# Leaving out the nine identity products per pass in a four-stage recurrent kernel

## The chip, the cores and the metric

The kernel runs on one core of a Trainium2 chip. The metric is the device time of one execution in microseconds. Time before the change: 4627.35 us, the median of 3 runs (4625.21 to 4628.95).

## What is computed

The input x has 4 sequences of 1024 tokens and 512 features. Four layers follow each other, each added to the stream:

```
x = x + rnn(x)        # h_t = tanh(x_t Wx + b + h_(t-1) Wh), 512 wide
x = x + ssm(x)        # conv over 4 taps, projections, softplus/tanh, a scan with 64 states, Wo
x = x + lstm(x)       # A = x_t Wx + b + h_(t-1) Wh (2048 wide), sigmoid/sigmoid/sigmoid/tanh gates
x = x + adapted(x)    # x times (base layer + low-rank part made from the condition vector)
```

Both the RNN and the LSTM are strictly sequential over 1024 tokens. All is float32; the recurrent weights and states are split into two float16 parts each.

## The kernel before

The 1024 tokens are cut into 32 chunks of 32 tokens (CT = 32, NCH = 32), and the four layers form a pipeline over chunks. A pass i handles chunk i in the RNN, chunk i-1 in the state-space layer ("mid"), chunk i-2 in the LSTM and chunk i-3 in the output layer; `chunk_work(i)` says which of them run. There are 35 passes, 0 to 34. Passes 0 to 3 are written out, passes 4 to 29 stand in a hardware loop of two passes an iteration (`pipeline`, `eng.Fori`, line 226 in the trace), so that 12 jumps back lie between them, and passes 30 to 34 are written out again. The LSTM runs in passes 2 to 33, the RNN in 0 to 31. Passes 2 to 31 are the 30 that run both; the windows below are taken from them.

Inside a pass every engine goes through the same 32 steps, one token of RNN and LSTM each. On TensorE a step s is, in program order:

- the LSTM products (L898): 64 matrix instructions with 256 moving columns, four at a time in column tiles. The first half waits for `lstm_h_ready0`, the rest for `lstm_h_ready1`, that is for VectorE's h of the step before (L753);
- the RNN products (L926): 32 instructions, behind `rnn_h_ready`;
- a filler that depends on s: the output layer (L938, steps 1, 2, 6, 13), the transposition of the next chunk (L1003, step 0), the state-space projections (L957, steps 3 to 5; those of step 4 wait for the convolution made on ScalarE and GpSimd), the RNN's input products (L1009, steps 7 to 10), the identity products (L972, steps 11, 30, 31), the state-space output (L977, step 12, behind `y_ready`), and the LSTM's input products (L991, steps 14 to 29).

TensorE, ScalarE, VectorE and GpSimd are joined by semaphores alone; there is no planner, the order is the one written by hand. VectorE transposes the LSTM's sums out of PSUM (L716), reduces them (L722), ScalarE makes the gates (L491) and tanh of the cell (L496), and VectorE makes products, cell and h (L728 to L753). In step 11 VectorE also runs the state-space scan, which waits for GpSimd. At the end of a pass each engine waits for a `go` from the SyncE queue (`next_chunk`).

The identity products multiply the 128 x 128 identity by itself into the fourth quarter of `psS`, which nothing reads:

```
HOLD_STEPS = [11, 30, 31]
...
if s in HOLD_STEPS:
    for _ in range(3):
        mm(psS[:, 3 * TOK:4 * TOK], ident[:, :], ident[:, :], start=True, stop=True)
```

They have no wait of their own, nobody waits for them, and they are issued in all 35 passes, also where the LSTM or the RNN is not at work. A float32 product is recorded as two matrix instructions and two weight loads.

Of the kernel before, what the change touches and what calls it, by code (L numbers as in the profile page):

```python
# [18 lines left out]
TOK = NB * CT  # L19
# [25 lines left out]
OUT_STEPS = [1, 2, 6, 13]  # L45
CONV_STEPS = [0, 1, 2, 2]
SSM_STEP = 3
HOLD_STEPS = [11, 30, 31]
L0_STEP = 7
RECIP_STEP = 7  # L50
RECIP_CUTS = [0, 40, 88, TOK]
# [25 lines left out]
def resid_stack_kernel(nc, x, cond, l0_Wx, l0_Wh, l0_b, conv_b, Wp, bp, Ws, bs, A_log, dt_log, Wo, bo,  # L77
                       l2_Wx, l2_Wh, l2_b, base, w1, b1, w2, b2, ln_g, ln_b, out):
    ctx = ExitStack()
    with ctx:  # L80
        def sb(name, shape, dt=F32):
            return ctx.enter_context(nc.sbuf_tensor(name, shape, dt))

        def pb(name):
            return ctx.enter_context(nc.psum_tensor(name, [P, 512], F32))
# [34 lines left out]
        ident = sb("ident", [P, P])  # L120
# [9 lines left out]
        def hidden(v):  # L130
# [53 lines left out]
        psL0, psL1, psR, psOut, psX, psS, psA, psB = [pb(n) for n in  # L184
            ("ps_lstm0", "ps_lstm1", "ps_rnn", "ps_out", "ps_x", "ps_ssm", "ps_lstm_in_a", "ps_lstm_in_b")]
# [643 lines left out]
        def _(pe):  # L829
            mm = nc.tensor.matmul  # L830
# [38 lines left out]
            for q in range(W2R):  # L869
# [4 lines left out]
                for k in range(KB):  # L874
                    for c in range(NQ):
                        last = mm((psA, psB)[q % 2][QC * c:QC * c + NB, 0:wd], hmT[:, k, :], w2s[q % 2][:, k, wd * c:wd * (c + 1)],
                                  start=(k == 0), stop=(k == KB - 1), tile_position=(0, QC * c))
# [11 lines left out]
            def body(_i, par, _known, w, p):  # L889
                S, S_last = sets[par], sets[1 - par]  # L890
                for s in range(CT):
# [26 lines left out]
                    if w["rnn"]:  # L918
# [4 lines left out]
                        for k in range(KB):  # L923
                            for e in range(2):
                                for j in range(NQ):
                                    last = mm(psR[QC * j:QC * j + LO + NB, 0:RW], hrs[:, k, :], whr[:, k, e, j, :],  # L926
                                              start=(k == 0 and e == 0), stop=(k == KB - 1 and e == 1), tile_position=(0, QC * j))
# [3 lines left out]
                    if w["out"] and s in OUT_STEPS:  # L931
# [5 lines left out]
                        for n in range(NB):  # L937
                            last = mm(psOut[CT * n:CT * (n + 1), :], x3s[1 - par][:, k, :, n], layer[:, n, k, :],  # L938
                                      start=(k == 0), stop=(k == KB - 1), tile_position=(0, CT * n))
# [8 lines left out]
                    if w["mid"] and SSM_STEP <= s < SSM_STEP + 3:  # L948
# [5 lines left out]
                        for k in range(KB):  # L954
# [3 lines left out]
                                      start=(k == 0), stop=(k == KB - 1))  # L958
                        if c == 1:
                            last.then_inc(S["ssm_mm"], 1)  # L960
                    if w["l0"] and L0_STEP <= s < L0_STEP + KB:
# [5 lines left out]
                            last = rnn_in(mm, wxr, xT[1 - par], psI, s - L0_STEP, k)  # L967
                        if s == L0_STEP + KB - 1:
                            last.then_inc(S["l0_mm"], 1)
                    if s in HOLD_STEPS:  # L970
                        for _ in range(3):
                            mm(psS[:, 3 * TOK:4 * TOK], ident[:, :], ident[:, :], start=True, stop=True)  # L972
                    if w["mid"] and s == WO_STEP:
                        pe.wait_ge(S["y_ready"], 1)
                        for b in range(KB):
# [3 lines left out]
                    if w["mid"] and s >= L2_STEP:  # L979
                        for u in range(L2_MM * (s - L2_STEP), min(L2_MM * (s - L2_STEP + 1), L2_ALL)):  # L980
# [7 lines left out]
                            if g >= 2 and b == 0 and k == 0:  # L988
# [3 lines left out]
                                      start=(k == 0), stop=(k == KB - 1))  # L992
                            if b == KB - 1 and k == KB - 1:
                                last.then_inc(S["l2_mm"], 1)
                next_chunk(pe, "pe")

            pipeline(pe, body)


# [74 lines left out]
```

## Time and profile before

| | us |
|---|---|
| median of 3 runs | 4627.35 |
| the profiled execution | 4620.95 |
| its span, first to last instruction | 4618.9 |
| TensorE products, busy | 3707.8 (80%) |
| TensorE weight loads, busy | 2997.8 (65%) |
| VectorE busy | 3678.6 (80%) |
| ScalarE busy | 1530.7 (33%) |
| GpSimd busy | 1283.4 (28%) |
| mean granted TensorE clock | 0.960 of full |

The profile is of one execution. Busy shares say how much an engine did, not whether it set the time. The granted clock is a share of TensorE's full 2.4 GHz; 0.5 is 1.2 GHz, and a value between them for a stretch means that part of it was at either. The timeline merges the instructions of one line that follow each other, so that a step's 64 LSTM products are one row; "idle before" is the idle time of the engine before the first of them, with what ended it. A row of the windows view gives, for a stretch A:B, its length, then busy us and number of instructions of TensorE's products, its weight loads, VectorE, ScalarE and GpSimd, then the granted clock, the share of the DMA engines and GB/s. A window of a step reaches from the start of its LSTM products to the start of the next ones.

### The profile page before, as it was taken

The numbers are of one execution on the slowest core, as the hardware profiler recorded it, in microseconds if no ns is written. First come the engines' busy times: TensorE is split into PE (matmuls) and PEld (weight loads), VectorE is DVE, ScalarE is ACT, GpSimd is POOL, SyncE is SP. The second block draws the span as 40 slices with busy tenths as digits, with TensorE's granted clock in tenths as the row PEclk, the third lists the DMA queues.
The fourth block names the chain that finished last, engine by engine and source line by source line (L and its number), as shares of the span: only waits on it lengthen the run. The fifth ranks groups of instructions, "written<-read, shape, count | busy, mean of one in ns | idle before, by whom it ended". The sixth has DMA issues, their size and how long they took to land.

```text
span 4618.9 us, 252593 instructions
## 1 busy us (share of the span) xinstructions
PE 3707.8 (80%) x106846; PEld 2997.8 (65%) x106846; DVE 3678.6 (80%) x20952; ACT 1530.7 (33%) x6667; POOL 1283.4 (28%) x4520
## 2 busy tenths in 40 slices
PE   4557888888888888888888888888888888888875
PEld 4246667676666666666666666666666766666653
DVE  5337888888888888888888888888888888888866
ACT  0013333333333333333333333333333333333321
POOL 0023332223333323233332223333223233333221
PEclk6579999999999999999999999999999999999999
DMA  4300000000000000000000000000000000000000
GB/s 152 117 4 6 8 6 8 9 8 6 9 8 7 8 9 8 7 9 8 9 6 9 8 8 7 8 9 8 7 8 9 6 8 9 8 4 6 6 5 7
DMA packets 28394, 64.27 MB, mean 14 GB/s; under 512 B 11068, under 2 KB 11708, under 8 KB 26120
## 3 DMA queue, kind: packets, MB, share of 16 engines
q1 hardware_dynamic: 27144, 46.99, 3.2%
q8 instruction: 860, 14.09, 1.3%
q14 instruction: 390, 3.19, 0.2%
HBM read 38.45 MB, written 8.39 MB: 10 GB/s over the span
## 4 chain that ended last, share of the span: by engine, by line
DVE 39%; PE 33%; ACT 10%; POOL 8%; issue 7%; DMA 1%; SPq 1%; DVEq 0%; POOLq 0%; ACTq 0%
PE ps_lstm L898 29%; DVE lstm_sums L716 10%; DVE lstm_arg L722 6%; DVE lstm_h_scaled L745 4%; ACT lstm_gates_2c L491 4%; ACT lstm_tanh_c L496 3%; DVE lstm_gates_2c L733 3%; POOL stage L378 3%; DVE lstm_ig_fc L728 2%; POOL stage L379 2%; DVE lstm_h_parts L753 2%; DVE rnn_h_parts L817 2%; DVE lstm_h_parts L749 2%; DVE rnn_arg L781 2%; DVE lstm_o_scaled L737 2%
## 5 line engine op out<-in xcount | busy, mean ns | idle before, releaser
L898 PE MATMUL ps_lstm<-lstm_Wh_parts,lstm_h_parts 128*20 128x256 f16 x65536 | 2039.9, 277 | 660.4 <-DVE lstm_h_parts L753 615.5
L898 PEld LDWEIGHTS ps_lstm<-lstm_Wh_parts,lstm_h_parts 128*20 128x20 f16 x65536 | 1508.2, 92 | 1182.8 <-DVE lstm_h_parts L753 932.7
L716 DVE STREAM_TRANSPOSE lstm_sums<-ps_lstm 128x256 f32<-128x256 f32 x2048 | 913.0, 446 | 180.7 <-PE ps_lstm L898 135.3
L491 ACT ACTIVATE lstm_gates_2c<-lstm_arg 128x32 f32<-128x32 f32 x2048 | 470.9, 230 | 1660.8 <-DVE lstm_arg L722 1660.0
L353 POOL COPY lstm_sums<-lstm_in 128x32 f32<-128x32 f32 x2048 | 412.5, 211 | 1408.0 <-DVE lstm_arg L722 1394.2
L926 PE MATMUL ps_rnn<-rnn_Wh_parts,rnn_h_parts 128*20 128x128 f16 x32768 | 651.1, 222 | 73.6 <-DVE rnn_h_parts L819 71.0
L926 PEld LDWEIGHTS ps_rnn<-rnn_Wh_parts,rnn_h_parts 128*20 128x20 f16 x32768 | 552.9, 93 | 117.6 <-DVE rnn_h_parts L819 97.9
L722 DVE TENSOR_REDUCE lstm_arg<-lstm_sums 128x32 f32<-128x96 f32 x2048 | 535.6, 262 | 106.7 <-DVE lstm_o_scaled L737 0.6
L496 ACT ACTIVATE lstm_tanh_c<-lstm_gates_2c 128x8 f32<-128x8 f32 x2048 | 413.1, 202 | 392.5 <-DVE lstm_gates_2c L733 384.8
L516 ACT ACTIVATE rnn_h<-rnn_arg 128x16 f32<-128x16 f32 x1024 | 221.1, 216 | 929.6 <-DVE rnn_arg L781 929.6
L817 DVE TENSOR_SCALAR rnn_h_parts<-rnn_h 128x16 f16<-128x16 f32 x1024 | 237.7, 232 | 291.1 <-ACT rnn_h L516 291.1
L728 DVE SCALAR_TENSOR_TENSOR lstm_ig_fc<-lstm_gates_2c 128x16 f32<-128x16 f32 x2048 | 368.8, 180 | 31.1 <-ACT lstm_gates_2c L491 31.0
L753 DVE TENSOR_TENSOR lstm_h_parts<-lstm_h_scaled,lstm_h_parts 128x8 f16<-128x8 f32 x2048 | 358.3, 175 | 37.4 <-DVE lstm_h_parts L749 2.4
L775 DVE STREAM_TRANSPOSE rnn_sums<-ps_rnn 128x128 f32<-128x128 f32 x1024 | 315.2, 308 | 62.9 <-PE ps_rnn L926 62.8
L733 DVE SCALAR_TENSOR_TENSOR lstm_gates_2c<-lstm_ig_fc 128x8 f32<-128x8 f32 x2048 | 364.1, 178 | 0.5 <-DVE lstm_h_scaled L745 0.2
L745 DVE TENSOR_TENSOR lstm_h_scaled<-lstm_o_scaled,lstm_tanh_c 128x8 f32<-128x8 f32 x2048 | 341.8, 167 | 3.4 <-DVE lstm_ig_fc L728 0.5
L737 DVE TENSOR_SCALAR lstm_o_scaled<-lstm_gates_2c 128x8 f32<-128x8 f32 x2048 | 340.0, 166 | 2.6
L365 POOL COPY rnn_sums<-rnn_in 128x16 f32<-128x16 f32 x512 | 100.5, 196 | 832.1 <-DVE rnn_arg L781 604.2
L749 DVE TENSOR_TENSOR lstm_h_parts<-lstm_o_scaled,lstm_tanh_c 128x8 f16<-128x8 f32 x2048 | 328.3, 160 | 0.3 <-issue 0.2
L991 PE MATMUL ps_lstm_in_a<-x,lstm_Wx 128*128 128x128 f32 x2048 | 298.2, 289 | 0.0
L991 PE MATMUL ps_lstm_in_b<-x,lstm_Wx 128*128 128x128 f32 x2048 | 296.5, 288 | 0.0
L365 POOL COPY rnn_sums<-stage 128x16 f32<-128x16 f32 x512 | 100.5, 196 | 653.0 <-DVE rnn_arg L781 586.2
(156 smaller groups left out, 3474.7 us busy)
## 6 DMA issues: line engine op xcount, KB each, us to landing
stage<-in_L_cond_w SPq DMA_DIRECT2D x8, 2048.0 KB, 8.0
x_rows<-in_x SPq DMA_DIRECT2D x32, 256.0 KB
out<-out_rows SPq DMA_DIRECT2D x128, 64.0 KB, 1.9
stage<-in_L_cond_Wh SPq DMA_DIRECT2D x1, 4096.0 KB, 12.7
lstm_Wx<-in_L_cond_Wx SPq DMA_DIRECT2D x1, 4096.0 KB, 13.3
stage<-in_L_cond_Wh SPq DMA_DIRECT2D x1, 1024.0 KB, 5.7
rnn_Wx<-in_L_cond_Wx SPq DMA_DIRECT2D x1, 1024.0 KB, 7.9
stage<-in_L_cond_w SPq DMA_DIRECT2D x1, 1024.0 KB, 15.1
```

Source lines behind the costliest of these rows:

```text
L491: A.activation(gate[h][:, 0:G, :].rearrange("p g q -> p (g q)"), arg[h][:, :, :].rearrange("p g n -> p (g n)"), ACT.Tanh, scale=gate_scale ...
L496: A.activation(tc[h][:, :], cell[h], ACT.Tanh, scale=0.5).then_inc(S[f"lstm_tanhc{h}"], 1)
L716: return mark(V.transpose(tr[h][s % 2][:, :, 0:QC], psL[h][:, 0:HW].rearrange("p (g c) -> p g c", c=QC)))
L722: V.tensor_reduce(arg[h][:, :, :], three.rearrange("p g s n -> p g n s"), AX.X, ALU.add).then_inc(S[f"lstm_summed{h}"], 1)
L728: return mark(V.scalar_tensor_tensor(out=prod[h][:, :, :], in0=gate[h][:, 0:2, :], scalar=1.0, in1=gate[h][:, G - 1:G + 1, :], op0=ALU.add ...
L733: V.scalar_tensor_tensor(out=cell[h], in0=prod[h][:, 1, :], scalar=0.5, in1=prod[h][:, 0, :], op0=ALU.mult, op1=ALU.add).then_inc(S[f"lstm ...
L737: return mark(V.tensor_scalar(o_s[h][:, :], gate[h][:, 2, :], 1.0, H_SCALE, ALU.add, ALU.mult))
L745: at = mark(V.tensor_tensor(half(hl, h)[:, :, s, :], o3, t3, ALU.mult))
L753: V.tensor_tensor(half(hls, h)[:, :, LO:LO + NB], half(hl, h)[:, :, s, :], half(hls, h)[:, :, 0:NB], ALU.subtract).then_inc(S[f"lstm_h_rea ...
L898: ins = mm(psL[h][QC * j:QC * j + LO + NB, 0:HW], hls[:, k, :], whl[:, k, h, e, j, :], start=(k == 0 and e == 0), stop=(k == KB - 1 and e ...
L926: last = mm(psR[QC * j:QC * j + LO + NB, 0:RW], hrs[:, k, :], whr[:, k, e, j, :], start=(k == 0 and e == 0), stop=(k == KB - 1 and e == 1) ...
L991: last = mm((psA, psB)[g % 2][:, TOK * b:TOK * (b + 1)], w_, x2[:, k, :, :].rearrange("p t n -> p (t n)"), start=(k == 0), stop=(k == KB - 1))
```

## The change

The nine identity products of each pass, three in each of steps 11, 30 and 31, are left out, and the constant with them. Nothing else changes.

```
-HOLD_STEPS = [11, 30, 31]
...
-                    if s in HOLD_STEPS:
-                        for _ in range(3):
-                            mm(psS[:, 3 * TOK:4 * TOK], ident[:, :], ident[:, :], start=True, stop=True)
```

## Rows read from the trace of the kernel before

**Rows 1.** The page, parts 1 and 2: busy us; clock in tenths.
```profile
PE 3707.8 (80%) x106846; PEld 2997.8 (65%) x106846; DVE 3678.6 (80%) x20952; ACT 1530.7 (33%) x6667; POOL 1283.4 (28%) x4520
...
PEclk6579999999999999999999999999999999999999
```

**Rows 2.** The page, parts 4 and 5: chain by engine, costliest group.
```profile
DVE 39%; PE 33%; ACT 10%; POOL 8%; issue 7%; DMA 1%; SPq 1%; DVEq 0%; POOLq 0%; ACTq 0%
...
L898 PE MATMUL ps_lstm<-lstm_Wh_parts,lstm_h_parts 128*20 128x256 f16 x65536 | 2039.9, 277 | 660.4 <-DVE lstm_h_parts L753 615.5
```

**Rows 3.** Timeline of TensorE, an ordinary step (start us, us, line).
```profile
2050.71 1.93 PE L898 MATMUL ps_lstm<-lstm_Wh_parts,lstm_h_parts 128*20 128x256 f16 x64 [0.33 <-DVE lstm_h_parts L753]
...
2054.51 1.93 PE L898 MATMUL ps_lstm<-lstm_Wh_parts,lstm_h_parts 128*20 128x256 f16 x64 [0.33 <-DVE lstm_h_parts L753]
```

**Rows 4.** Timeline of TensorE, around steps 11, 12 and 30 of the same pass.
```profile
2015.36 0.94 PE L972 MATMUL ps_ssm<-ident 128*128 128x128 f32 x6
2018.66 0.62 PE L898 MATMUL ps_lstm<-lstm_Wh_parts,lstm_h_parts 128*20 128x256 f16 x16 [2.37 <-DVE lstm_h_parts L753]
2019.60 1.49 PE L898 MATMUL ps_lstm<-lstm_Wh_parts,lstm_h_parts 128*20 128x256 f16 x48 [0.32 <-DVE lstm_h_parts L753]
...
2093.15 1.93 PE L898 MATMUL ps_lstm<-lstm_Wh_parts,lstm_h_parts 128*20 128x256 f16 x64 [0.56 <-DVE lstm_h_parts L753]
```

**Rows 5.** Answer on line 972: durations in ns; nobody waited.
```profile
L972 PE MATMUL ps_ssm<-ident x630: 275/275/582, 238.8 to 4615.7; 128*128 128x128 f32 x158
...
who waited for it (us, times):
```

**Rows 6.** Timeline of TensorE in the first pass (clock halved).
```profile
285.45 1.04 PE L926 MATMUL ps_rnn<-rnn_Wh_parts,rnn_h_parts 128*20 128x128 f16 x32 [1.48 <-DVE rnn_h_parts L819]
286.42 1.65 PE L972 MATMUL ps_ssm<-ident 128*128 128x128 f32 x6
```

**Rows 7.** Chain of work that ended last, at its end.
```profile
4612.57 0.87 PE ps_ssm L972 x6
4613.44 1.03 PE ps_out L938 x8
```

**Rows 8.** Timeline of TensorE at a loop jump.
```profile
1959.80 0.28 PE L972 MATMUL ps_ssm<-ident 128*128 128x128 f32 x1
1963.47 3.46 PE L898 MATMUL ps_lstm<-lstm_Wh_parts,lstm_h_parts 128*20 128x256 f16 x64 [3.39 <-issue]
```

**Rows 9.** Answer on line 226: TensorE's sequencer branches (ns).
```profile
L226 PEldq COMPARE_BRANCH  x13: 76/4255/4780, 892.5 to 4089.3; - x13
```

**Rows 10.** Windows, step 12 of passes 4, 29 and 31.
```profile
681.76:687.26 5.50, 5.17 (x106) 4.12 (x106) 4.35 (x27) 2.38 (x9) 1.03 (x4) 0.69 0.01 1
...
4012.51:4016.87 4.36, 3.63 (x104) 2.94 (x104) 3.87 (x24) 2.37 (x9) 1.02 (x4) 1.00 0.00 0
...
4273.61:4279.16 5.55, 5.08 (x104) 3.75 (x104) 4.05 (x24) 0.98 (x5) 1.02 (x4) 0.69 0.02 4
```

**Rows 11.** Windows, step 0 of passes 6, 12, 20 and 21.
```profile
896.70:901.60 4.90, 3.60 (x104) 3.08 (x104) 2.48 (x16) 0.77 (x4) 0.42 (x2) 1.00 0.03 10
...
1698.15:1704.22 6.07, 6.07 (x104) 4.74 (x105) 3.00 (x18) 0.77 (x4) 0.45 (x3) 0.53 0.03 8
...
2762.48:2767.67 5.19, 4.85 (x105) 3.67 (x105) 2.53 (x15) 0.77 (x4) 0.42 (x2) 0.72 0.03 9
2895.75:2899.55 3.80, 3.46 (x104) 2.97 (x104) 3.33 (x21) 0.98 (x5) 1.64 (x9) 1.00 0.03 6
```

**Rows 12.** Timeline of TensorE, the product that waits for the convolution.
```profile
1986.09 1.09 PE L957 MATMUL ps_ssm<-stage,ssm_Wp 128*64 128x128 f32 x8 [2.15 <-POOL stage L371]
```

**Rows 13.** Windows, step 5 of passes 28 and 29.
```profile
3850.80:3856.25 5.45, 5.04 (x105) 3.77 (x104) 3.09 (x19) 0.98 (x5) 0.62 (x3) 0.69 0.02 3
3982.77:3986.57 3.80, 3.39 (x105) 2.92 (x104) 2.94 (x18) 0.99 (x5) 0.62 (x3) 1.00 0.02 6
```

**Rows 14.** Timeline of TensorE, near the end, steps with only an LSTM.
```profile
4593.72 1.93 PE L898 MATMUL ps_lstm<-lstm_Wh_parts,lstm_h_parts 128*20 128x256 f16 x64 [1.87 <-DVE lstm_h_parts L753]
```

## Prediction

> **What bounds the kernel now.** I read the page first for busy shares: TensorE 80%, VectorE 80%, neither full, and a granted clock that is 9 tenths or more after the opening [rows 1]. Two engines at 80% with nothing near 100% is the sign of a chain that hands work back and forth. The chain of waits says so: VectorE 39%, TensorE 33%, ScalarE 10% of the span, and the costliest group is the LSTM product of L898, whose 660.4 us of idle time before it end, for 615.5 us, with VectorE's h parts (L753) [rows 2]. So the time is the recurrence, one step after the other: products, transpose, reduce, tanh, cell, h, products.
>
> Then the timeline of TensorE, to see what lies in a step. In an ordinary one the LSTM products start at 2050.71, take 1.93 us, and the next ones start at 2054.51: 3.80 us a step. A filler (L991, the next pass's input product) ends 0.33 us before the next start [rows 3]. TensorE's work behind the LSTM products is thus hidden, with 0.33 us to spare. What sits on the path is the 1.93 us, and that is the part which depends on TensorE's clock.
>
> **What the change removes.** Three identity products in each of steps 11, 30 and 31 of each of 35 passes: 630 recorded matrix instructions (2 x 9 x 35), which is six for each group of three; such a six takes 0.94 us at full clock, from the start of its first to the end of its last in the merged timeline, and 1.65 us at half clock [rows 5, 6]. Nobody reads their output: no engine waits for them [rows 5]. Nothing is added or moved, no wait changes.
>
> **Direct cost, step by step.** Steps 30 and 31: the products end and TensorE idles 0.56 us until the h parts come [rows 4]. Removing them makes that wait about 1.4 us and moves nothing: 0. Step 11: TensorE idles 2.37 us behind them [rows 4]; VectorE is held there by the scan of the state-space layer, which waits for GpSimd. Removing 0.94 us of TensorE work in front moves nothing either: 0. In the last pass three of them stand in the chain that ends last, 0.87 us in front of the last output product [rows 7]: -0.87. In the first pass, where the clock is halved and there is no LSTM, a group takes 1.65 us where the step before had 1.48 us of idle [rows 6]: 0.17 us too much, once or twice, bounds 0 and -0.34, taken -0.2.
>
> The loop jump: every second pass TensorE's sequencer spends 4.26 us (median) in the branch [rows 9], and the LSTM products start when it ends. Counted back from the start at 1963.47, that branch began near 1959.1, when the last identity products (the final one starts 1959.80 [rows 8]) had hardly begun. So the sequencer runs ahead of the engine, and only the issue of the twelve instructions (six loads, six products), not their 0.9 us, can delay it. Bounds: 0 and -0.85 us at each of 12 jumps, -10.2. I take -0.1 x 12 = -1.2, near the first end, since the branch already overlaps the products.
>
> **Indirect cost: the clock.** This is where I expect the time. The identity products are the only TensorE work in some gaps, and the windows show what follows a gap. In passes 2 to 31, step 12 takes 4.36 or 4.37 us at granted clock 1.00 in 25, and 5.49 to 5.55 us at 0.69 in 5 (the ones at 681.76, 814.59, 951.29, 4142.74 and 4273.61, of which first and last stand in the rows) [rows 10]. A clock of 0.69 over the step means that part of it ran at 1.2 GHz rather than 2.4 GHz; the price is 5.49 - 4.36 = 1.13 us. What TensorE did before the fall is the same gap of 2.2 to 2.4 us after the step 11 products. So with the products in place this gap already costs a fall in 5 passes of 30. Without them the gap is 2.37 + 0.94 = 3.31 us.
>
> What follows a gap of that size? The gap at the loop jump is 3.39 us in [rows 8], and 11 of 12 jumps show a lower clock in step 0: 5.19 us at 0.72 where the pass without a jump has 3.80 us at 1.00; the one that escaped was the first, 4.90 us at 1.00 [rows 11]. The gap of 2.15 us in front of a product that waits for the convolution [rows 12] is followed by a slow step 5 (5.45 us at 0.69 against 3.80) in ten of the eleven even passes from 1188.72 to 3850.80 and in none of the odd ones between them [rows 13]. So after 2.2 us the clock falls sometimes, after 3.4 us nearly always. At 3.31 us I take it that step 12 falls in all 25 passes that now escape: 25 x 1.13 = +28.3.
>
> How long the slow stretch lasts is the next question. The cover in step 12 is thinner than in step 0: 0.32 us idle inside its LSTM products [rows 4]. The jump at 1698.15 shows what a slow stretch that is followed by another costs: 6.07 us at 0.53 [rows 11]. At step 12 a second stretch would fall on step 13, an ordinary step, and the nearest price of an ordinary step at the lower clock is step 5's, 5.45 - 3.80 = 1.65 us [rows 13]. Bounds: never, 0; always, 30 x 1.65 = 49.5. Eleven jumps fell and one had a second stretch, but there TensorE is busier after the fall; I take one pass in three, 10 x 1.65 = +16.5.
>
> At the jump the gap grows from 3.4 to about 4.3 us, so the fall lies earlier and more of step 0 is slow. Bounds: 0 and 6.07 - 5.19 = 0.88 us at 12 jumps, 10.6 [rows 11]. I take 0.3 x 12 = +3.6. Steps 30 and 31 where no jump follows have 1.4 us of idle in 3.8, less than a step with only an LSTM product (1.87 us idle in the last passes [rows 14]), where the page's clock still shows 9 tenths [rows 1]: 0.
>
> A rule of the Trainium skill bears on this. The row shows a slow step 0 of 5.19 us against 3.80, +1.39 us [rows 11]. The page "TensorE: Matmul & The Clock Gate", section "HAM oscillation — how this bites in real kernels", says that an idle wait between bursts returns the engine to half rate, so that the next burst starts cold each time; the row agrees that the fall follows the gap. By the page's half rate the whole LSTM product of step 12 would take 1.93 us more, 25 x 1.93 = 48 us instead of the 28.3 above (an estimate from the page's rule and [rows 3]), and the sum would be 4693. The rows decide for 1.13, since only part of the step is slow.
>
> **Sum.** -0.9 - 0.2 - 1.2 + 28.3 + 16.5 + 3.6 = +46.1 us. The profiled execution had 4620.95 us (span 4618.9 and 2.05 around it): 4667. The median of the three runs is 6.4 us above it, so on that footing 4627.35 + 46.1 = 4673.4 us, +1.0%.
>
> **The rivals.**
> *No change.* The identity products keep nothing up: the fall at step 12 depends on where the gap happens to lie against the clock's own rhythm, and as many passes fall as now. For it: 5 passes fall with the products in place, and the last odd passes before the end do not fall at the conv gap of the same size. Against it: the 3.4 us gaps. Then only -0.9 - 0.2 - 1.2 is left: 4625 us.
> *Faster.* The sequencer is held by the queue behind the identity products, so that each branch begins the whole 0.85 us sooner: 12 x 0.85 = 10.2, with the last pass 11.1 to 11.3: 4616 us. For it: the branch starts about when the first of them does. It decides only if step 12 does not fall in more than about ten further passes (10 x 1.13 = 11.3); from there the clock wins.
> *Much slower.* The slow state feeds itself: step 13 falls in every pass and step 0 is slow throughout, 28.3 + 49.5 + 10.6 - 2.3 = +86: 4713 us. A step with only an LSTM, as in the last pass but one, could also stay slow. Against it: all but one of the falls at jumps were over within the step.
>
> **How the numbers follow.** Forecast, step 12 falls nearly everywhere and step 13 in part: 0.74. Much slower: 0.10. No change: 0.09. Faster: 0.07. The likeliest case's own range is 4650 to 4700: below, step 13 never falls and the jump costs nothing, 4673 - 20 = 4653; above, half of the passes more, +1.65 x 15 = 25. The range for 8 in 10 goes from 4645 to 4706, which leaves out the no-change and the faster case and most of the much slower one. 0.2% of the time, 9 us, is about what a measurement of this kernel can tell from no change. Slower by more than that: 0.74 + 0.10 = 0.84. Within: 0.09 and some of the faster case (its 11 us is just outside), 0.10. Faster: 0.06.
>
> **What the profile of the changed kernel would show.** Right: L972 gone; the idle time before step 12's LSTM products 3.2 to 3.3 us; granted clock about 0.7 in the windows of step 12 in at least 25 passes of 30 with 5.5 us each; a slow step 13 in some; the mean granted clock down from 0.960; the pair of passes between jumps longer by about 3.5 us. Wrong: step 12 at 4.36 us and clock 1.00 in most passes (then the gap is still covered); a loop gap shorter by 0.8 us (then the queue held the branch); step 12 slow but step 11's stall on GpSimd swallowing the loss later, so that the pass is no longer; or step 13 slow everywhere.

## The result

The changed kernel takes 4667.23 us, the median of 4 runs (4662.29 to 4668.49), against 4626.28 us before (4 runs, 4619.68 to 4628.95). The ratio is 1.0089, 95% interval 1.0071 to 1.0106: slower by 0.9%, about 41 us. The profiled execution took 4668.49 us, its span is 4666.7 us, 47.7 us more than before.

From the page of the changed kernel: busy time, the clock in 40 slices, the chain by engine, and the costliest group (all lines behind the diff have moved up by one, so L897 is the L898 of [rows 2]).

```profile
PE 3672.4 (79%) x106216; PEld 2959.1 (63%) x106216; DVE 3679.2 (79%) x20952; ACT 1532.0 (33%) x6667; POOL 1284.4 (28%) x4520
...
PEclk6569999999999999999999999999999999999999
...
DVE 37%; PE 36%; ACT 10%; POOL 8%; issue 7%; DMA 1%; SPq 1%; DVEq 0%; POOLq 0%; ACTq 0%
...
L897 PE MATMUL ps_lstm<-lstm_Wh_parts,lstm_h_parts 128*20 128x256 f16 x65536 | 2068.3, 279 | 739.4 <-DVE lstm_h_parts L752 674.7
```

TensorE does less (630 recorded matrix instructions gone, two for each of 315 products) and yet has a larger share of the chain, 36% against 33% in [rows 2]; the same 65536 LSTM products take 2068.3 us instead of 2039.9. The 40 slices hardly show it; the mean granted clock does, 0.944 against 0.960. The idle time before the products grew too, by 79 us, so the clock is not all.

To see where the time lies, one window for each step s of the 30 passes, and the sums over them. The windows of step 12 of the changed kernel, four of 30 and the sum:

```profile
958.38:964.60 6.22, 6.21 (x105) 4.68 (x106) 4.53 (x27) 2.51 (x10) 1.12 (x5) 0.53 0.01 4
1091.97:1096.34 4.37, 3.64 (x105) 2.95 (x105) 3.88 (x24) 2.38 (x9) 1.03 (x4) 1.00 0.02 4
...
2036.74:2041.89 5.15, 4.81 (x104) 3.42 (x104) 4.05 (x24) 2.38 (x9) 1.02 (x4) 0.73 0.02 5
2167.62:2173.11 5.49, 5.17 (x104) 4.18 (x104) 4.43 (x27) 2.38 (x9) 1.03 (x4) 0.69 0.01 3
...
sum 154.88, PE 142.48 PEld 109.79 DVE 124.82 ACT 70.91 POOL 31.43; mean PE 4.75 PEld 3.66 DVE 4.16 ACT 2.36 POOL 1.05
```

19 of 30 are at a lower clock (5 before), and the sum is 154.88 us against 136.62 in the same view of the kernel before [rows 10]: +18.3. The sum before:

```profile
sum 136.62, PE 116.68 PEld 94.30 DVE 118.62 ACT 69.99 POOL 30.84; mean PE 3.89 PEld 3.14 DVE 3.95 ACT 2.33 POOL 1.03
```

Step 0, the step behind the loop jump, one window at a jump, one without, and the sum of 30:

```profile
1981.37:1988.74 7.37, 6.36 (x105) 4.87 (x106) 3.01 (x18) 0.77 (x4) 0.42 (x2) 0.54 0.03 8
2115.82:2119.62 3.80, 3.47 (x104) 2.95 (x104) 3.33 (x21) 0.98 (x5) 1.63 (x9) 1.00 0.03 6
...
sum 159.98, PE 135.51 PEld 108.22 DVE 94.92 ACT 28.32 POOL 35.37; mean PE 4.52 PEld 3.61 DVE 3.16 ACT 0.94 POOL 1.18
```

Against 131.18 before: +28.8, and 28.2 of it at the 12 jumps (7.1 to 8.2 us each; 4.9 to 6.1 before, [rows 11]). The sum of step 31, which holds the jump, fell from 148.41 to 140.81: -7.6. Step 0 before, then step 31 before and in the changed kernel:

```profile
sum 131.18, PE 119.61 PEld 97.19 DVE 90.70 ACT 26.86 POOL 34.45; mean PE 3.99 PEld 3.24 DVE 3.02 ACT 0.90 POOL 1.15
...
sum 148.41, PE 97.25 PEld 81.75 DVE 109.50 ACT 70.45 POOL 20.99; mean PE 3.24 PEld 2.73 DVE 3.65 ACT 2.35 POOL 0.70
...
sum 140.81, PE 71.33 PEld 59.53 DVE 109.36 ACT 70.56 POOL 20.97; mean PE 2.38 PEld 1.98 DVE 3.65 ACT 2.35 POOL 0.70
```

Steps 4 and 5 gave +4.8 and -0.7. With 2.3 us before the first LSTM product, 2.6 in passes 32 and 33 and -1.0 at the end that is 47.5 of the 47.7; the other steps nearly cancel.

The timeline of TensorE at one jump of the changed kernel says what step 0 is made of:

```profile
1977.30 0.62 PE L925 MATMUL ps_rnn<-rnn_Wh_parts,rnn_h_parts 128*20 128x128 f16 x32
1981.37 2.06 PE L897 MATMUL ps_lstm<-lstm_Wh_parts,lstm_h_parts 128*20 128x256 f16 x34 [3.45 <-issue]
1984.44 1.88 PE L897 MATMUL ps_lstm<-lstm_Wh_parts,lstm_h_parts 128*20 128x256 f16 x30 [1.01 <-issue]
1985.91 1.27 PE L925 MATMUL ps_rnn<-rnn_Wh_parts,rnn_h_parts 128*20 128x128 f16 x32
1987.11 1.70 PE L999 MATMUL ps_x<-ident,x_rows 128*128 128x128 f32 x8
```

There is a second hole. Behind the 34th of the 64 LSTM products TensorE idles 1.01 us, waiting for nothing that the profile shows ("issue"). It is at the 34th at all 12 jumps, 0.9 to 2.3 us long, and at none in the kernel before, where the 64 stand in one row [rows 8]. Nearly half of the extra time lies at the jump, with a cause that the prediction had not looked at.

### The profile page after: what moved, and what is told of

It is laid out like the page before. It is cut to its first block, busy times and chain, and to the rows that moved or that the text cites. A ratio compares the mean times of both kernels' runs of the same rounds, so it can differ in the third digit from the quotient of the medians.

```text
span 4666.7 us, 251333 instructions
## 1 busy us (share of the span) xinstructions
PE 3672.4 (79%) x106216; PEld 2959.1 (63%) x106216; DVE 3679.2 (79%) x20952; ACT 1532.0 (33%) x6667; POOL 1284.4 (28%) x4520
## 4 chain that ended last, share of the span: by engine, by line
DVE 37%; PE 36%; ACT 10%; POOL 8%; issue 7%; DMA 1%; SPq 1%; DVEq 0%; POOLq 0%; ACTq 0%
PE ps_lstm L897 31%; DVE lstm_sums L715 10%; DVE lstm_arg L721 6%; DVE lstm_h_scaled L744 4%; ACT lstm_gates_2c L490 4%; ACT lstm_tanh_c L495 3%; DVE lstm_gates_2c L732 3%; POOL stage L377 2%; POOL stage L378 2%; DVE lstm_h_parts L752 2%; DVE lstm_ig_fc L727 2%; DVE rnn_h_parts L816 2%; DVE lstm_h_parts L748 2%; PE ps_rnn L925 2%; DVE lstm_o_scaled L736 2%
## 5 line engine op out<-in xcount | busy, mean ns | idle before, releaser
L897 PE MATMUL ps_lstm<-lstm_Wh_parts,lstm_h_parts 128*20 128x256 f16 x65536 | 2068.3, 279 | 739.4 <-DVE lstm_h_parts L752 674.7
L897 PEld LDWEIGHTS ps_lstm<-lstm_Wh_parts,lstm_h_parts 128*20 128x20 f16 x65536 | 1520.2, 93 | 1273.7 <-DVE lstm_h_parts L752 989.8
L925 PE MATMUL ps_rnn<-rnn_Wh_parts,rnn_h_parts 128*20 128x128 f16 x32768 | 665.1, 225 | 76.0 <-DVE rnn_h_parts L818 74.5
L925 PEld LDWEIGHTS ps_rnn<-rnn_Wh_parts,rnn_h_parts 128*20 128x20 f16 x32768 | 565.9, 95 | 121.3 <-DVE rnn_h_parts L818 101.5
```

Source lines behind the costliest of these rows:

```text
L897: ins = mm(psL[h][QC * j:QC * j + LO + NB, 0:HW], hls[:, k, :], whl[:, k, h, e, j, :], start=(k == 0 and e == 0), stop=(k == KB - 1 and e ...
```

## The experiments

Each time is a median of 5 or 11 runs beside 9 to 21 runs of the kernel before on the same chip. Windows, timelines and counts of slow passes (a pass is slow in a step where the clock granted in that window is below full) come from the one profiled execution of each kernel. The identity products feed nothing, so none of these kernels leaves out part of the computation. "Short products" are identity products with 4 moving columns, put into the set-up in front of the wait for the low-rank factors' DMA:

```
+            for _ in range(N):
+                mm(psS[:, 3 * TOK:3 * TOK + 4], ident[:, :], ident[:, 0:4], start=True, stop=True)
             pe.wait_ge(d_xab, 16 * 2 * NQ * NB)
```

**36 short products ahead of the loop (e1_pad36).** The changed kernel with N = 36, as many products as the change takes out of passes 0 to 3.

> The changed kernel, with 36 short identity products (4 moving columns) put into the set-up before the loop, behind the low-rank weight products where TensorE waits for a DMA: as many as the change takes out of passes 0 to 3. The loop body stays without any. In the changed kernel every step 0 behind a loop jump stops after its 34th LSTM product for 0.9 to 2.3 us, idle that is put down to issue; the kernel before never does. Placement theory: that stop is instruction supply, and depends on where the loop begins in the program; with 36 products put back ahead of it the stop is gone, step 0 behind a jump falls from 7.1-8.1 us to 5.0-6.1, and the time falls by 12 x 1.5 to 2.2 = 18 to 26 us, to 4641-4650. Cover theory (the missing products in step 31 let the gap grow and the clock fall earlier, and nothing else): the stop stays, step 0 stays above 7 us, and the time stays at 4667 within 4.

4630.08 us (11 runs, 4623.93 to 4636.65) against 4620.71 (21 runs), ratio 1.0020, 1.0011 to 1.0029. The timeline at a jump:

```profile
1429.95 0.62 PE L928 MATMUL ps_rnn<-rnn_Wh_parts,rnn_h_parts 128*20 128x128 f16 x32
1434.08 3.58 PE L900 MATMUL ps_lstm<-lstm_Wh_parts,lstm_h_parts 128*20 128x256 f16 x64 [3.51 <-issue]
1437.46 0.65 PE L928 MATMUL ps_rnn<-rnn_Wh_parts,rnn_h_parts 128*20 128x128 f16 x32
```

The hole in the LSTM products is gone, step 0 at the jumps is 5.2 to 6.1 us, and three quarters of the loss with it: 1.0020 in place of 1.0089. It went below the range of the placement theory (4641 to 4650): step 31 also lost 10.2 us against before. The cover theory is out for step 0. What stays is step 12: 24 of 30 passes at a lower clock, +20.0 us. The sums of its step 0 and step 12:

```profile
sum 135.33, PE 126.22 PEld 103.25 DVE 91.74 ACT 27.32 POOL 34.86; mean PE 4.21 PEld 3.44 DVE 3.06 ACT 0.91 POOL 1.16
...
sum 156.61, PE 144.66 PEld 112.43 DVE 125.64 ACT 70.96 POOL 31.56; mean PE 4.82 PEld 3.75 DVE 4.19 ACT 2.37 POOL 1.05
```

**9 short products (e2_pad9).** The changed kernel with N = 9.

> The changed kernel with 9 short identity products put ahead of the loop instead of 36. Placement theory with a fixed size of what is there after a jump: 9 products are 36 instructions of loads and products if each float32 product counts four times, so 18 LSTM products: the stop moves from behind product 34 to behind product 52 (43 if a product counts twice). It comes about 0.5 us later behind the jump and more of it is covered: step 0 6.5 to 7.6 us, the time 4655 to 4667. Cover theory: the stop stays behind product 34, or has nothing to do with a number of products; 4667.

4662.76 us against 4620.71, 1.0085 (1.0071 to 1.0099). The time lies in the expected range, but not for the reason given. At a jump:

```profile
1436.39 0.61 PE L900 MATMUL ps_lstm<-lstm_Wh_parts,lstm_h_parts 128*20 128x256 f16 x16 [3.80 <-issue]
1439.64 2.74 PE L900 MATMUL ps_lstm<-lstm_Wh_parts,lstm_h_parts 128*20 128x256 f16 x48 [2.63 <-issue]
```

The hole moved by 18 products, as said, but to the front: behind the 16th, not the 52nd, and it is longer (2.0 to 2.6 us). So 9 products ahead are 36 instructions, and they take from what is there after a jump, they do not add to it. I had the direction wrong. That fits a block with fixed borders: the more code lies ahead of the loop, the later in its block the loop begins, and the fewer of its instructions came with the first fetch.

**Identity products out of passes 0 to 3 alone (e3_head_out).**

```
-                    if s in HOLD_STEPS:
+                    if s in HOLD_STEPS and _known not in (0, 1, 2, 3):
```

> The kernel before with the identity products left out in passes 0 to 3 alone; the loop and the passes behind it keep all of them. Placement theory: the loop now begins where it does in the changed kernel, so the stop behind product 34 appears in the kernel that has its cover: step 0 behind a jump 6 to 7.5 us rather than 5.0-5.3, 12 x 1 to 2 us, and passes 2 and 3 cost 5.6 us more as in the changed kernel: 4640 to 4658. Cover theory: only passes 2 and 3 change, 4627 + 5.6 = 4632.

4638.17 us against 4620.71, 1.0040 (1.0026 to 1.0054). The hole behind the 34th product is there (1.24 us), in a loop that has all its identity products:

```profile
1434.39 2.10 PE L898 MATMUL ps_lstm<-lstm_Wh_parts,lstm_h_parts 128*20 128x256 f16 x34 [2.72 <-issue]
1437.72 1.88 PE L898 MATMUL ps_lstm<-lstm_Wh_parts,lstm_h_parts 128*20 128x256 f16 x30 [1.24 <-issue]
```

That is a little below the expected range and well above the rival's 4632: steps 5 and 31 gave 9.5 and 7.7 us back, while step 12 cost 8.1, with 13 slow passes, two of them passes 2 and 3. Step 0 sums to 160.68 us, as in the changed kernel, while the gap before it at the jumps is only 2.4 to 3.0 us. The missing cover in steps 30 and 31 is not needed for a step 0 above 7 us.

**Only step 11's products, only those of steps 30 and 31 (e4_hold11, e5_hold3031).** `HOLD_STEPS = [11]` with N = 24, and `HOLD_STEPS = [30, 31]` with N = 12, so that the loop begins at the same place in both as before. Where it ends still moves, since its body is shorter: by 48 and by 24 instructions (four for each identity product: two matrix instructions and two weight loads).

> The three products of step 11 kept in all passes, those of steps 30 and 31 left out, and 24 short ones put ahead of the loop so that it begins where it did before. It asks what the products of steps 30 and 31 are worth apart from placement. If they keep the clock up at the jump, step 0 is slower than before by 0.5 to 1.5 us at 12 jumps: 4633 to 4645. If they do nothing, or if their absence lets the jump start 0.6 us earlier at no cost (step 31 was 0.63 us shorter in the changed kernel), 4619 to 4629. Step 12 is slow in 4 to 8 passes of 30 either way, as before (5).

> The products of steps 30 and 31 kept in all passes, those of step 11 left out, and 12 short ones put ahead of the loop so that it begins where it did before. With placement equal the changed kernel was 9.4 us slower than before (4630.1 against 4620.7), and by steps its trace showed +20 us in step 12 (24 slow passes of 30 against 5) against -10 in step 31. If step 12's fall is due to the missing products of step 11 alone, this one shows 20 to 28 slow passes in step 12 and +18 to +24 us there, and is slower than before by 15 to 25 us where step 31 stays as before, or by 8 to 12 if the jump is shorter here too. Rival: the falls at step 12 come from where the whole pass lies against the clock's changes, and without a shorter step 31 they stay at 5 to 10: within 5 us of before.

Without steps 30 and 31: 4624.86 us against 4620.71, 1.0010 (1.0001 to 1.0019). Step 0 +2.6, step 12 +2.3 with 7 slow passes, step 31 +3.5, where the branch takes 4.52 us instead of 4.26; the time is that of the second case, products that do nearly nothing. The gap at the jump is 4.2 to 5.0 us here, and step 0 at the jumps grew by only 0.17 us each. Without step 11: 4651.13 against 4626.89, 1.0061 (1.0047 to 1.0075), and step 12 has 23 slow passes of 30. The windows of passes 6 to 8 and the sum for step 12 of the latter:

```profile
958.09:964.22 6.13, 6.13 (x104) 4.54 (x104) 4.52 (x27) 2.42 (x10) 1.03 (x5) 0.53 0.00 1
1091.55:1095.91 4.36, 3.64 (x104) 2.95 (x104) 3.87 (x24) 2.38 (x9) 1.02 (x4) 1.00 0.01 4
1227.46:1232.55 5.09, 4.74 (x106) 3.38 (x106) 4.06 (x24) 2.38 (x9) 1.02 (x4) 0.75 0.01 2
...
sum 160.04, PE 149.93 PEld 114.12 DVE 126.64 ACT 70.88 POOL 31.37; mean PE 5.00 PEld 3.80 DVE 4.22 ACT 2.36 POOL 1.05
```

160.04 - 136.62 = +23.4 us: the three products of step 11 are what keeps the clock up in step 12, and they carry nearly all that the nine are worth. The rival that the falls need a shorter step 31 is out: step 31 is 3.3 us longer in sum here. The idle time before step 12's products is now 3.10 or 3.23 us, from pass to pass, where it was 2.23 or 2.37 [rows 4]. The count of slow passes wanders: 4 to 13 of 30 in the seven kernels that keep the step 11 products in the loop (5, 13, 7 and 10 where the gap is as before), 19 to 24 in the five that do not. The two groups stay apart, but a difference of a few passes inside one says little.

**64 short products (e6_pad64).** The changed kernel with N = 64.

> The changed kernel with 64 short identity products ahead of the loop. 9 products moved the stop behind the jump from the 34th LSTM product to the 16th, 18 products of 2 instructions each for 9 x 4 = 36 instructions; 36 products moved it to where the 90th product of the step would be. If the supply comes in fixed blocks of 256 instructions (16384 bytes, as the packets of the instruction queue are), 64 products are one whole block and the stop is behind product 34 again, the time 4655 to 4670. Rival: what counts is only how much code lies ahead, or that something was put there at all; then the stop is elsewhere or gone and the time near 4630.

4662.29 us against 4626.89, 1.0082 (1.0068 to 1.0096), and the hole is behind the 34th product again:

```profile
1445.01 2.10 PE L900 MATMUL ps_lstm<-lstm_Wh_parts,lstm_h_parts 128*20 128x256 f16 x34 [3.78 <-issue]
1447.89 1.88 PE L900 MATMUL ps_lstm<-lstm_Wh_parts,lstm_h_parts 128*20 128x256 f16 x30 [0.79 <-issue]
```

64 x 4 = 256 instructions are one period. With the others: 34 products left without padding, 34 - 18 = 16 with 9, 34 - 72 + 128 = 90 with 36, 34 - 128 + 128 = 34 with 64. The kernel before has the same 90 as e1_pad36, and in it the hole is in the RNN products, behind 64 + 26, at the one jump that did not fall in clock (the 4.90 us at 1.00 of [rows 11]); at the jumps that fell, in both kernels, none can be seen:

```profile
896.70 1.92 PE L898 MATMUL ps_lstm<-lstm_Wh_parts,lstm_h_parts 128*20 128x256 f16 x64 [3.22 <-issue]
898.45 0.56 PE L926 MATMUL ps_rnn<-rnn_Wh_parts,rnn_h_parts 128*20 128x128 f16 x26
900.30 0.28 PE L926 MATMUL ps_rnn<-rnn_Wh_parts,rnn_h_parts 128*20 128x128 f16 x6 [1.30 <-issue]
```

**More cover (e7_cover).** The other way: in the loop passes 5 products ahead of the wait for the convolution, 6 in step 11, and 3 long ones ahead of the jump.

```
+                        if c == 0 and _known is None:
+                            for _ in range(5):
+                                mm(psS[:, 3 * TOK:4 * TOK], ident[:, :], ident[:, :], start=True, stop=True)
                         if c == 0:
                             pe.wait_ge(S["conv_ready"], KB)
...
-                        for _ in range(3):
-                            mm(psS[:, 3 * TOK:4 * TOK], ident[:, :], ident[:, :], start=True, stop=True)
+                        wide = _known is None and par == 1 and s == CT - 1
+                        for _ in range(6 if _known is None and s == 11 else 3):
+                            if wide:
+                                mm(psS[:, :], ident[:, :], layer[:, 0, 0, :], start=True, stop=True)
+                            else:
+                                mm(psS[:, 3 * TOK:4 * TOK], ident[:, :], ident[:, :], start=True, stop=True)
```

> The kernel before with more cover, in the loop passes only, so that the loop begins where it did: 5 identity products in step 4 ahead of the wait for the convolution, 6 instead of 3 in step 11, and in step 31 of the odd pass, ahead of the jump, 3 products with 512 moving columns instead of 128. Clock theory: gaps of 2.15, 2.4 and 3.4 us shrink to about 0.6, 1.4 and 1.4; the falls at steps 5, 12 and 0 vanish, 11 x 1.4 at the jumps, 13 x 1.2 to 1.6 at step 5 and 5 x 1.1 at step 12, in all 36 to 42 us: 4580 to 4586. Rival: the long products delay the branch or the first LSTM products behind it, or the sequencer's queue, and step 31 or 5 grows by more than step 0 gains: 4615 to 4640.

4590.34 us (4585.70 to 4595.38) against 4626.89, ratio 0.9927, 0.9914 to 0.9941: faster than both kernels, 36.5 us below the kernel before, and 4 us above the expected range. The timeline at a jump, then step 0 and the sum of step 5:

```profile
1415.49 2.84 PE L977 MATMUL ps_ssm<-layer_plus_2I,ident 128*128 128x512 f32 x6
1419.00 1.93 PE L898 MATMUL ps_lstm<-lstm_Wh_parts,lstm_h_parts 128*20 128x256 f16 x64 [0.66 <-issue]
1420.75 0.56 PE L926 MATMUL ps_rnn<-rnn_Wh_parts,rnn_h_parts 128*20 128x128 f16 x26
1422.15 0.28 PE L926 MATMUL ps_rnn<-rnn_Wh_parts,rnn_h_parts 128*20 128x128 f16 x6 [0.84 <-issue]
```

```profile
1419.00:1423.86 4.86, 3.69 (x105) 3.10 (x105) 2.44 (x15) 0.77 (x4) 0.42 (x2) 1.00 0.05 12
```

```profile
sum 115.22, PE 103.00 PEld 88.64 DVE 90.65 ACT 29.34 POOL 18.26; mean PE 3.43 PEld 2.95 DVE 3.02 ACT 0.98 POOL 0.61
```

No step 0 at a jump and one step 5 (of pass 30, behind the loop) is at a lower clock now, 11 and 13 before. Step 5 gave -16.4 us, step 4 -3.0, step 0 -6.6, step 31 -7.0. The last is not the clock's: the branch takes 3.58 us instead of 4.26, and the loop's end has moved by 64 instructions; with the same cover and another end the next two runs have branches of 4.20 and 3.81 us. That leaves some 29 of the 36 us to the cover. Step 12 gave only -1.2: the doubled cover, a gap of 1.6 to 1.7 us, left 4 slow passes where 5 had been, all four of them inside the loop. Step 0 kept more than the expectation left it, 4.4 to 5.0 us at full clock, because the hole behind the 90th product is now in the open.

**More cover and 45 or 59 short products (e8_cover_pad45, e9_cover_pad59).**

> The kernel with more cover and 45 short identity products ahead of the loop, which by blocks of 256 instructions puts the loop's first instruction at the start of a block (180 instructions further than before: 90 products of 2 left become 128). The stop that stood behind product 90 of step 0 in one pass of the kernel before cannot occur in step 0. If the jump fetches one block before it goes on, nothing else changes: within 3 us of the kernel with more cover alone. If what lies behind in the block also sets the length of the branch, step 31 changes by up to 0.8 us at 12 jumps, 10 us either way.

> More cover, with 59 short identity products ahead of the loop. The last expectation had the sign of the count wrong: products ahead of the loop take from what is left of the block behind the jump, so 45 left nothing (step 31 with the jump took 9.8 to 10.4 us, two fetches in a row). With 59, 90 - 118 + 128 = 100 products of the loop's first block are left, more than the 96 LSTM and RNN products of step 0, so the stop of 0.7 to 1.1 us behind the 90th is gone from the RNN products. The end of the loop moves by 300 instructions against the kernel before, that is 44 of a block of 256. Over ten kernels the branch took 4.1 to 5.1 us where that end was shifted by -48 to 0 and 3.3 to 4.15 where by +36 to +184 (counted modulo 256). Block theory: branch 3.3 to 4.1, no stop, 4580 to 4591, at best 8 us below more cover alone (4590). Rival: placement matters only where the stop hits the LSTM products, since RNN products have slack: the same time within 3 us.

With 45: 4652.80 us against 4626.89, 1.0060 (1.0046 to 1.0073), slower than before in spite of all its cover.

```profile
1430.07 2.84 PE L979 MATMUL ps_ssm<-layer_plus_2I,ident 128*128 128x512 f32 x6
1438.12 3.60 PE L900 MATMUL ps_lstm<-lstm_Wh_parts,lstm_h_parts 128*20 128x256 f16 x64 [5.21 <-issue]
```

I had used the direction that the run with 9 had already refuted. By the right count 90 - 90 = 0 products of the first block are left, and that is what stands here: 5.21 us of idle in place of 0.66, since the first LSTM product of the loop comes with the second fetch. 12 x 3.9 = 47 us, the step 31 sum being 188.04 against 141.47 with more cover alone. All 12 step 0 are at a lower clock again, which costs 9.6 us more. It is the worst place of those run.

With 59: 4587.52 us against 4625.48, 0.9917 (0.9903 to 0.9931). The hole behind the 100th product, as computed, can be seen at 4 of the 12 jumps (0.15 to 0.28 us), and step 0 lost 4.3 us against more cover alone, but step 31 gave 1.9 back. The two intervals overlap; the 2.8 us between them are not shown to be a gain.

**46 short products in the kernel before (e10_pad46).**

> The kernel before, all nine identity products kept, with 46 short ones ahead of the loop: 126 products of the first block are left behind the jump, and the end of the loop is shifted by 184 of 256 instructions, the same as in the kernel with 36 products ahead and none in the loop, whose branch took 3.3 to 3.9 us. Theory that the place of the loop's end in its block sets the length of the branch: 3.3 to 3.9 us instead of 4.1 to 4.8, 12 x 0.65 = 8 us less in step 31, of which the clock at step 0 and 12 may give or take some: 4612 to 4622. Rival: the branch is shorter in those kernels because the loop holds fewer instructions or something else that was changed in each: branch 4.1 to 4.8 and 4623 to 4630.

4622.65 us against 4625.48 (11 and 15 runs), 0.9992, 0.9982 to 1.0002. TensorE's branches of the kernels, each line min/median/max in ns: the changed kernel, then only step 11's, then this one:

```profile
L225 PEldq COMPARE_BRANCH  x13: 76/3810/4073, 899.2 to 4135.1; - x13
```

```profile
L226 PEldq COMPARE_BRANCH  x13: 76/4524/5104, 899.7 to 4097.5; - x13
```

```profile
L226 PEldq COMPARE_BRANCH  x13: 76/3462/3822, 890.3 to 4079.9; - x13
```

The branch is shorter as forecast (3.46 against the 4.26 us of [rows 9]) with the same loop body, and step 31 lost 9.9 us, while step 12 gave 5.4 back (10 slow passes instead of 5). That execution's span is 7.8 us below the one of the kernel before, as forecast; but it is the fastest of the 11, and the medians differ by only 2.8 us, between the two expected ranges. So the length of the branch follows the place, and a gain in time is not shown.

## Why the prediction was right, and which of its steps were not

The direction and the size hold (forecast 4673, range 4645 to 4706, measured 4667). The working does not hold as well as the total.

*Steps 11, 30 and 31 are off the path:* right. No step with or without them changed by its own TensorE work: step 30, and step 31 where no jump follows, take 3.80 us in both kernels. The end gave -1.0 us, -0.87 said. The 0.2 us said for the first pass can't be seen: the first LSTM product comes 368.1 to 371.8 us into the span over the twelve profiled executions, with no order by the products left out.

*Step 12 falls in clock, at 1.13 us each:* right in mechanism, shown by the run that leaves out step 11's products alone. Mis-sized: not all 25 further passes fell but 14 (19 of 30), and with placement restored 19 (24 of 30). The price was near the 1.13 us said in 13 of the 19 (5.09 to 5.55 against 4.36 us, 0.7 to 1.2) and 1.8 us in the other six (6.12 to 6.21 us, at 0.53), so 18.3 us came of 14 further passes where 1.13 each would give 15.8.

*A second slow stretch on step 13 in one pass of three, +16.5:* wrong. Step 13 is slow in none (in one pass each of the runs with 9 and 64 short products, +1.4 and +1.5 us). Steps 12 and 13 together were forecast at 44.8 us and gave 18.3.

*The branch begins 0.1 us sooner:* right, 0.08 us (its start lies 2.17 instead of 2.25 us behind the start of step 31's LSTM products). But the branch was also 0.45 us shorter in the median, and step 31 gave -7.6 where -1.2 stood. The faster rival had 10.2 us there, for another reason.

*The jump costs 0.3 us more, +3.6:* this step failed. It reads the gap as TensorE's idle time and the clock behind it, and takes the code behind the jump as given. Step 0 gave +28.8, and in the run where the place of the loop's beginning is restored it gave +4.2. The rest is the hole in the instruction supply. The gap did not grow to 4.3 us either: its median over the jumps went from 3.35 to 3.66 us, because the branch became shorter; in the run with step 11's products alone, where the branch takes 4.52 us, it is 4.53. Each step 0 at a jump grew by 2.35 us where the hole has 1.4 in the mean; with it the clock is lower, 0.50 to 0.62 where it was 0.70 to 0.74 in ten of twelve. That TensorE stays low for longer because it idles once more is likely, but only argued.

So the 0.9% are the sum of three things. With the loop's beginning in its old place the change costs 0.20% (0.11 to 0.29), 9 us, and that is a balance: +20 in step 12 for the products that are gone, -10 in step 31 for a branch that is shorter because the loop ends elsewhere. The other 0.7%, some 32 us, come from where 36 products fewer in the written-out passes put the loop's beginning. The 26.5 us that steps 12 and 13 did not cost were made up by 19 more than forecast at the jump and some 9 in steps 4 and 5, ahead of the first LSTM product and in passes 32 and 33; the total was hit with the wrong terms, by luck.

The rivals: "no change" is excluded by the slow passes of step 12, "much slower" by step 13. What stays open is why 24 passes fall in step 12 and not 30, and which of the gaps of 1.6 to 2.4 us are followed by a fall; no run here settles that.

## What to carry to other kernels

Look at what TensorE does in a gap before you call its work useless: leaving out products that nothing reads and nobody waits for cost 24 us in one place (step 11) and 4 in another (steps 30 and 31), of which some 3 each are the place of the loop's end, and more of them in the right gaps gained some 29. When a change takes instructions out of code ahead of a hardware loop, hold the place of the loop with as many dummy instructions before you judge the change; here the place of its beginning alone cost 32 us, more than the products' 20. An instruction taken out of the loop's body moves its end too, and that can hide a loss: here by 10 us. A hole marked "issue" at the same product after each jump is the sign of it.

## What the runs showed of the hardware

A loop jump of TensorE, back over two passes of work, takes 3.3 to 5.1 us; the last branch, which is not taken, 0.08 us (76 ns). On VectorE, ScalarE and GpSimd the same branch has a median of 63, 45 and 45 ns in the changed kernel, taken in 12 of 13 cases. After a jump TensorE's instructions come in blocks of 256: the hole moves by 2 products (4 instructions) for each float32 product put ahead, and returns after 64. A block is 16384 bytes if an instruction is 64 bytes, and the instruction queue moved 14.09 MB in 860 packets, 16.4 KB each:

```profile
q8 instruction: 860, 14.09, 1.3%
```

The Trainium skill says this in "Runtime: NRT & Kernel Launch", section "Instruction fetch mechanics": the instruction memory is refilled in blocks of 256 instructions, and a taken branch whose target isn't there waits for a DMA. The runs agree, and give the price. The Trainium skill's figure for a compare-and-branch in "Advanced Engine Details and Errata", section "Control Flow Timing", is about 108 ns; no branch here has it: TensorE's takes 76 ns where it is not taken and 30 times the figure or more where it is.

The hole is 0.8 to 2.6 us long if the first block has 16 to 34 LSTM products, 0.7 to 1.3 behind the 90th where TensorE is at full clock (hidden or up to 0.15 where it is not), up to 0.3 behind the 100th, and about 4 us if nothing of the first step is in it. The time of the branch itself follows the place of the loop's end. Counted against the kernel before, in instructions modulo 256, the end lies at -48, -24, -12 and 0 in the kernels whose medians are 4.52, 4.62, 4.20 and 4.26 us, and at 40 to 184 in those with 3.46 to 3.81 us. Five of them begin the loop at the same place, and the order holds among these (4.52, 4.62 and 4.26 us at -48, -24 and 0; 3.58 and 3.57 at 64 and 184). That a block on its way when the branch comes has to arrive first would explain it, but that is only argued.
